# One residual load is issued later in the SyncE queue of a fused AdaLN, SSM and FFN kernel

## The reference

```python
h = _layernorm(x) * (1 + ca) + sa
x = x + ga * ssm(h)          # projection to x, B, C, z, A; conv of 4 taps; decayed attention form; silu(z) gate; W_out
h = _layernorm(x) * (1 + cb) + sb
x = x + gb * ffn(h)          # silu(h W1) * (h W3), Walsh-Hadamard transform over 1024, W2
```

## Time and profile before

| what | value |
|---|---|
| median of 3 runs | 562.82 us |
| the profiled execution's own time | 562.82 us |
| its span | 561.0 us |
| TensorE busy | 551.6 us, 98% |
| VectorE busy | 471.9 us, 84% |
| ScalarE busy | 392.3 us, 70% |
| GpSimd busy | 256.8 us, 46% |
| granted TensorE clock, mean | 0.994 |

### The profile page before, as it was taken

How to read it: one execution, slowest core, us unless ns; L and a number is a source line. 1 busy time by engine, 2 the same in 40 slices (tenths; PEclk the granted TensorE clock), 3 DMA queues, 4 the chain that set the end, 5 groups by cost and what they waited for, 6 DMA issues and landing times.

```text
span 561.0 us, 18569 instructions
## 1 busy us (share of the span) xinstructions
PE 551.6 (98%) x6701; PEld 447.0 (80%) x6702; DVE 471.9 (84%) x746; ACT 392.3 (70%) x988; POOL 256.8 (46%) x523
## 2 busy tenths in 40 slices
PE   7999999999999999999999999999999999999997
PEld 4577787888778878788887888787788988889887
DVE  7899999999999999999999999999948637647343
ACT  2679898898898888988988989988723323333240
POOL 4854387576577577687678364656100000000000
PEclk9899999999999999999999999999999999999999
DMA  8636534433433535533533437456741042100101
GB/s 275 264 140 199 171 120 132 166 117 121 168 117 118 168 112 203 171 113 119 162 127 117 143 142 223 135 163 191 204 136 54 22 129 75 39 2 0 39 1 37
DMA packets 40816, 72.01 MB, mean 128 GB/s; under 512 B 4676, under 2 KB 12100, under 8 KB 40520
## 3 DMA queue, kind: packets, MB, share of 16 engines
q1 hardware_dynamic: 40776, 71.52, 40.0%
HBM read 57.34 MB, written 13.12 MB: 126 GB/s over the span
## 4 chain that ended last, share of the span: by engine, by line
PE 93%; DVE 2%; issue 2%; POOL 1%; DMA 1%; ACT 0%; SPq 0%; POOLq 0%; DVEq 0%; ACTq 0%
PE ps L355 20%; PE ps L357 20%; PE ps L356 20%; PE ps L530 9%; PE ps L512 5%; PE ps L574 5%; PE ps L549 4%; PE ps L565 4%; PE ps L640 2%; PE ps L449 1%; PE ps L377 1%; PE ps L407 1%; PE ps L421 1%; PE ps L650 1%; DMA u_sb<-in_u 1%
## 5 line engine op out<-in xcount | busy, mean ns | idle before, releaser
L1148 DVE SCALAR_TENSOR_TENSOR acc<-ps,cw_dve,acc 128x511 f32<-128x511 f32 (+2 forms) x384 | 257.7, 742 | 2.9 <-ACT acc L807 2.7
L839 ACT ACTIVATE decay<-sums,p_slot 128x128 f32<-128x128 f32 x512 | 161.1, 399 | 4.8 <-POOL sums L1436 2.1
L1432 POOL TENSOR_SCALAR_AFFINE_SELECT sums<-sums 128x512 f32<-128x512 f32 x128 | 82.4, 644 | 93.5 <-DMA sums<-running_sums 88.5
L807 ACT ACTIVATE acc<-ps,cw_act 128x512 f32<-128x512 f32 x128 | 93.1, 776 | 32.2 <-PE ps L574 30.1
L355 PE MATMUL ps<-ht_hi,wg_hi 128*128 128x512 f32 x256 | 107.1, 418 | 0.0
L356 PE MATMUL ps<-ht_lo,wg_hi 128*128 128x512 f32 x256 | 101.2, 395 | 0.0
L357 PE MATMUL ps<-ht_hi,wg_lo 128*128 128x512 f32 x256 | 101.1, 395 | 0.0
L1136 DVE TENSOR_TENSOR mix<-ps,decay 128x1024 f32<-128x1024 f32 x64 | 78.2, 1222 | 11.4 <-PE ps L530 10.2
L974 ACT ACTIVATE silu_sb<-ps 128x512 f32<-128x512 f32 x32 | 19.2, 599 | 77.8 <-PE ps L357 77.8
L1436 POOL TENSOR_SCALAR_AFFINE_SELECT sums<-sums 64x256 f32<-64x256 f32 x128 | 51.9, 405 | 29.7 <-POOL sums L1432 29.2
L1366 POOL TENSOR_TENSOR rstd<-vareps,minus_half 128x4 f32<-128x4 f32 x8 | 8.4, 1047 | 120.4 <-DVE vareps L1030 116.8
(11 more groups left out here) (142 smaller groups left out, 945.2 us busy)
## 6 DMA issues: line engine op xcount, KB each, us to landing
sums<-running_sums SPq DMA_DIRECT2D x128, 256.0 KB, 3.2
y_parts<-yt_sb SPq DMA_DIRECT2D x32, 256.0 KB, 2.0
wg_raw<-in_w_bc SPq DMA_DIRECT2D x8, 512.0 KB, 4.5
stage<-y_parts SPq DMA_DIRECT2D x16, 256.0 KB, 4.5
u_sb<-in_u SPq DMA_DIRECT2D x4, 512.0 KB, 4.3
stage<-in_w SPq DMA_DIRECT2D x1, 2048.0 KB, 13.2
x_channels<-acc SPq DMA_DIRECT2D x8, 256.0 KB, 2.6
ee<-decay_rows SPq DMA_DIRECT2D x8, 256.0 KB, 3.9
```

Of the source, the lines that this page charges most:

```text
L807: af(acc[:, b % 2, t, :], ps[:, PROJ_BANK[t], :], ACT.Identity, bias=cw_act[:, t, 1:2], scale=cw_act[:, t, 0:1]).then_inc(s[f"tap_a{t}"], 1)
L839: i = af(decay[:, j, c * P:(c + 1) * P], sums[:, j, c * P:(c + 1) * P], ACT.Exp, scale=-1.0, bias=p_slot[:, b * CH + c, j:j + 1])
L1148: stt(a[:, d:], ps[:, PROJ_BANK[t], 0:L - d], cw_dve[:, t, TAPS - 1 - d:TAPS - d], a[:, d:], ALU.mult, ALU.add).then_inc(s[f"taps{t}"], 1)
L1432: gp.affine_select(out=v, in_=v, compare_op=ALU.is_ge, fill=FAR, base=0, pattern=[[0, 2], [NS, 2], [1, P]], channel_multiplier=-1).then_in ...
```

## The change

The wait for `proj2` and the load of sequence 0's `u2` leave the last SyncE step, where they stood between the third sum load and the gate loads, and come right after that step, behind its fourth sum load. Nothing on another engine changes.

```diff
@@ SyncE, step(g, b, gr, last) @@
                 for j in range(3):
                     load_sum(g, b, j)
                 if last:
-                    sp.wait_ge(s["proj2"], NG * B)
-                    load(u2[:], u_b[0], "ld_res")
                     gate_loads()
                 if gr is not None:
                     store_y(gr, (b - 2) % B)
@@ SyncE, after the last step @@
             step(NG - 1, B - 1, NG - 1, last=True)
+            sp.wait_ge(s["proj2"], NG * B)
+            load(u2[:], u_b[0], "ld_res")
+
             def next_front(b):
```

## The result

The changed kernel takes 569.24 us (568.93 to 569.75, 4 runs) against 563.38 us (562.36 to 563.95, 4 runs) for the kernel before: a ratio of 1.0107, interval 1.0087 to 1.0127. It is slower by 5.9 us. The forecast was 3.8 us more, with a range up to 568.6, so the direction is right and the size is not. Measured once more (experiment 5) it was again 569.24, against 562.36: 1.0121, interval 1.0104 to 1.0138.

The account below looks back on a forecast made before the run. TensorE, busy for 98% of the span, was taken as the bound, waiting on VectorE at the hand-over to the FFN. 562.8 + 3.8 (late addition) - 0 (gates) = 566.6 us; 8-in-10 range 565.0 to 568.6.

Parts of the forecast that it names:

- The place of the loss: At the hand-over from SSM loop to FFN, VectorE's residual addition waits for the late u2 load: 3.8 us later.
- the gates' side: Gate loads freed of 512 KB ahead of them: gain taken as 0; as a rival 0.92 us gained, 561.9, chance 0.02.
- the 0.92 us ahead of the mix: VectorE's idle time before the mix at 389.08, put down to decays and not a DMA; bound on any gain.
- One to one behind the addition: VectorE's later steps and TensorE up to the FFN have no slack, so all move by the addition's 3.8 us.
- nothing measurable: Rival: a later TensorE wait for something that doesn't move covers the addition's delay; 563 us, chance 0.04.
- The landing: The u2 load, issued at 389.4 behind the fourth sum load, takes 5.2 us and lands at 394.6.
- The analog at 378.16: The same load before the change, 0.4 us behind a sum load, lands 1.4 us after the sums; gives 394.5.
- The bytes argument: Sums and u2 are the first 768 KB of a dense row of issues; today's first 768 KB land about 394.6.
- The clock: TensorE's granted clock in its new waits before the FFN: no term in the sum; rival of 2.2 us, chance 0.15.
- The rival's 568.8: Clock falls in TensorE's new gap, work runs at half speed: 2.2 us on top of 566.6, chance 0.15.
- The ring-order rival: Ring order or a light queue lets the u2 load land sooner: 564.6 to 565.5 us, chance 0.11.
- quick landing: The u2 load lands at 392.8, 3.4 us after issue like the lone one, costing 2.0: 564.8 us.

Follow-up runs that it names:

- experiment 5: The changed kernel itself measured again beside the kernel before, nothing altered: 569.24 us, ratio 1.0121.
- Experiment 1: Against the kernel before: load of u2 moved behind the gate loads and the store, but ahead of the fourth sum load's wait for decays; 562.77 us, ratio 1.0006.
- experiment 4: Against the changed kernel: load of u2 waits for the same decays but is issued ahead of the fourth sum load; 564.98 us, ratio 1.0052 to the kernel before.
- experiment 2: The changed kernel plus 18 and 8 unread matmuls that keep TensorE busy in its waits; 566.79 us, ratio 1.0075 to the kernel before.
- experiment 6: The changed kernel with nothing issued behind the u2 load until it lands, plus 12 and 8 unread matmuls in TensorE's waits; 565.89 us, ratio 1.0057.
- experiment 8: Against the changed kernel: load of u2 moved behind four more loads of sequence 1 (two ee, two xt); 572.18 us, ratio 1.0178 to the kernel before.
- experiment 3: The changed kernel with one more wait: SyncE issues nothing behind the u2 load until it has landed; 567.82 us, ratio 1.0099 to the kernel before.
- experiment 7: Against the changed kernel: behind the same decays, a plain 256 KB xt load goes before the u2 load, the sums after it; 566.99 us, ratio 1.0079.

## Why the prediction was wrong, step by step

**The place of the loss: right.** The load goes out behind the fourth sum load, the addition waits for it by name, nothing else moves by itself, and the gates' side gave nothing. Experiment 1 shows that the gates and the store, which the load also passes, cost nothing. Experiments 1, 4 and 5 together split the delay of 4.4 us: the wait for decays makes 1.5, and standing behind the broadcast of sums, once through the wait, makes the other 2.9. Two readings on the way were wrong and did no harm. VectorE does not work without a gap up to the end of `h2_low`; it waits for ScalarE ahead of both its last steps (0.57 us at 403.04). And the row of the 0.92 us ahead of the mix names no releaser, it says `issue`; it rules a DMA out no more than it shows decays.

**One to one behind the addition: right.** Experiments 2, 4 and 6 have the FFN late by what the addition is late, within 0.15 us; in 8 the clock's part comes on top. No cover was found, which disposes of the rival "nothing measurable".

**The landing: too small by 1.0 us.** The step "so I take 5.2 us to landing" measured 6.2 (6.0 in experiment 5). The analog at 378.16 had no loads issued behind it for 1.5 us, and 4.8 to 5.2 is what the load takes without them (experiments 6 and 3). With sums in front, loads behind cost another 0.8 to 1.4. The bytes argument, 768 KB moved by 394.6, took a broadcast and a plain load as equal; 6.0 to 6.2 us behind the one and 3.9 behind the other (experiment 7) show that they are not. This raised the delay from 3.8 to 4.65 us. By itself it would have given 567.5, inside the range.

**The clock: the step that failed.** The sum has no term for the clock: it stands at 0 there, and 2.3 to 2.7 us were measured. I wrote that a gap of this kind can lower the clock, priced it at 2.2 us, and gave it 0.15, since "there the small matmuls of the modulation preceded it, here the dense loop". The dense loop ahead of the gap didn't protect it. The clock fell in the profiles of the change, its repeat and experiments 3, 7 and 8, and it stayed up in 2 and 6, where the difference was work in the gaps. The price was about right: 2.4 us by experiment 2 against the changed kernel, 1.9 by experiment 6 against 3 (0.3 of it the landing), 2.3 to 2.7 in the profiles of the change. The rival's 568.8 is within 0.5 us of the measured 569.24, partly by luck, as it had the landing 1.0 us too short. The trace had spoken for it: my own working put two waits around 1.1 us of work, more idle time than the 1.5 us around the fall at the start. It even had the first wait too short, 1.6 us. These two rows of the kernel before give 2.1:

```profile
393.01 0.69 DVE L1156 TENSOR_TENSOR w_lo<-ps,w_hi 128x512 fp32r<-128x512 f32 x1
394.50 0.87 PE L549 MATMUL ps<-xds,b_tok 128*64 128x24 f32 x24
```

The transform needs the first of them, which would end at 393.70 + 3.8 = 397.5, and TensorE is done with its last work at 395.37. One fall at the start was thin evidence all the same: in the profiles of experiments 3 and 5 TensorE has the same wait of 1.46 us there and the clock stays at 1.00. So a gap of this length lowers it in some executions and not in others, which makes 0.15 too little, but would not have made it certain. The Trainium skill, page "TensorE: Matmul & The Clock Gate", Part 1, says that the throttled state is the default and that recent activity lifts it. The runs agree as far as they go: the clock fell in TensorE's waits (after 1.5 us of one in experiment 3, for example) although a dense loop stood before them, and stayed up where extra matmuls filled the time.

**The ring-order rival: half right.** Its quick landing did not come (6.2 us, not 3.4 to 3.9), yet what it rests on did show in experiment 4. By the Trainium skill, page "DMA: Bandwidth & Descriptors", section "Queues, rings and completion order", each engine consumes its descriptors in ring order. The 3.4 us of experiment 4 with five loads issued behind agree with it. The 0.8 to 1.4 us that loads behind add when the sums are in front do not follow from it, and neither does the `u2` load of 466.07 in the trace of before: with nothing in front and a 512 KB store issued 0.4 us behind, it takes 4.3 us to land (3.9 in the profile of the change), against the 3.4 of the lone one. No run here shows where that comes from.

## What to carry to other kernels

Before a DMA is moved down a queue, look for the first wait behind which it would then stand: the five DMAs ahead of that wait cost nothing here, the wait itself 1.5 us of delay, and the broadcast load behind it another 2.9. When a delay makes TensorE idle, price the delay and the clock together; if the trace holds even one gap of similar length with the clock falling in it, the fall is no remote case. Of the six profiles here with 2 us or more of new idle time and no extra matmuls (the change and experiments 3, 4, 5, 7 and 8) five have it. And a landing time is to be taken from a DMA with the same kind of load in front and behind, not only of the same size.

## What was not expected of the hardware

- Each landing time is from one trace, or from two or three where a range is given. A 512 KB load landed in 3.4 us with five loads issued behind it before it landed and none in front, in 3.9 us with a plain 256 KB load in front, in 4.8 to 5.2 us with a 256 KB broadcast of one HBM row to 128 partitions in front, and in 6.0 to 6.2 us with that broadcast in front and eight loads behind.
- 26 added matmuls that nobody reads made the changed kernel 2.4 us faster, as the granted clock stayed at 1.00 instead of 0.50.
- In the changed kernel TensorE had nothing to do from 395.7 on, and the granted clock was down by 398 and stayed at 0.50 until past 407, though TensorE was busy again from 402 on. How long TensorE had stood still when the clock fell differs: 1.5 us in experiment 3 and 3.7 us in experiment 8; in experiment 5 it was at 1.00 through a gap of 2.76 us and fell in the next one, and in experiment 4 a single gap of 2.05 us left it at 1.00 in the profiled execution.
